# Reordering the per-unit work of a patch-attention tokenizer: value quarters before the score sums

## The reference, cut to what matters

```
reduce = mean over the 16 pixels of a patch               # 256 patches per image
q = layernorm(reduce) @ Wq.T                              # one query per patch
k, v = layernorm(pixels) @ Wkv.T                          # 16 keys and values per patch
attn = softmax(q * scale . k over the 16 pixels)          # 8 heads
token = reduce + (sum over pixels of attn * v) @ proj_w.T + proj_b
```

## Time and profile before

| what | value |
|---|---|
| median of 3 runs | 897.04 us (896.9 to 900.0) |
| the profiled execution's own time | 897.0 us |
| its span, first to last instruction | 895.2 us |
| granted TensorE clock, mean | 0.994 |
| PE busy | 844.0 us, 94% |
| DVE busy | 722.9 us, 81% |
| POOL busy | 523.4 us, 58% (work almost only in the tokenizer) |
| ACT busy | 494.1 us, 55% |
| tokenizer | to about 575 us of the span |

### The profile page before, as it was taken

The page is one execution under the profiler, slowest core; times in us unless marked ns, Lnnn a source line. Parts: engine busy times, 40 slices in busy tenths (PEclk is TensorE's granted clock), DMA queues, the critical chain, the costliest instruction groups (busy, mean ns, idle before and its releaser), DMA issues.

```text
span 895.2 us, 23485 instructions
## 1 busy us (share of the span) xinstructions
PE 844.0 (94%) x9144; PEld 354.2 (40%) x9144; DVE 722.9 (81%) x1189; ACT 494.1 (55%) x782; POOL 523.4 (58%) x387
## 2 busy tenths in 40 slices
PE   5799999999999999999999999798999999999996
PEld 1134434334334433433433434254344444444442
DVE  5688788788788788788788788895878878778775
ACT  3545555555545545545545546357766666666662
POOL 2789989989989989989989984200112111111110
PEclk9999999999999999999999999899999999999999
DMA  9588998998998998998998955200000000000000
GB/s 370 164 233 244 245 280 230 251 273 230 251 275 230 250 273 224 258 272 232 249 272 233 251 144 131 60 3 2 1 12 13 24 13 13 25 12 13 24 13 35
DMA packets 70560, 141.60 MB, mean 158 GB/s; under 512 B 5440, under 2 KB 5440, under 8 KB 69440
## 3 DMA queue, kind: packets, MB, share of 16 engines
q1 hardware_dynamic: 70464, 140.21, 54.9%
HBM read 68.88 MB, written 4.19 MB: 82 GB/s over the span
## 4 chain that ended last, share of the span: by engine, by line
PE 83%; DVE 7%; POOL 3%; DMA 3%; issue 2%; ACT 1%; SPq 1%; POOLq 0%; DVEq 0%
PE ring L956 24%; PE bank_ms L928 12%; PE bank_sq L928 6%; PE qp L995 6%; PE ring L1215 5%; DVE sb_prodk L1357 4%; PE ring L1185 4%; PE bank_ms L1227 3%; PE qp L916 2%; PE qp L1170 2%; DMA sb_arena<-x 2%; PE bank_sq L1215 2%; PE ring L1130 1%; PE bank_ms L1222 1%; PE bank_ms L1185 1%
## 5 line engine op out<-in xcount | busy, mean ns | idle before, releaser
L956 PE MATMUL ring<-sb_arena,sb_wqkv 64*64 64x512 f32 x2048 | 255.1, 601 | 5.2 <-DVE sb_prodv L1388 3.7
L1357 DVE TENSOR_TENSOR sb_prodk<-ring,sb_qbuf 128x1024 f32<-128x1024 f32 x128 | 153.3, 1220 | 18.5 <-PE ring L956 15.4
L653 POOL TENSOR_TENSOR sb_parts_q<-sb_arena,sb_const 128x512 fp32r<-128x512 f32 x15 | 15.6, 1039 | 244.8 <-DVE sb_arena L1593 194.4
L1388 DVE TENSOR_TENSOR sb_prodv<-ring,sb_wbc 128x1024 f32<-128x1024 f32 x128 | 151.0, 1202 | 1.9 <-issue 1.9
L497 POOL TENSOR_TENSOR sb_rows<-sb_arena 128x2048 f32<-128x2048 f32 x31 | 141.8, 4575 | 16.5 <-DMA sb_arena<-x 16.5
L697 ACT ACTIVATE sb_xsq<-sb_arena 128x2048 f32<-128x2048 f32 x64 | 118.4, 1896 | 3.4 <-DMA sb_arena<-x 3.4
L995 PEld LDWEIGHTS qp<-sb_prodv,sb_tok_w 64*64 64x64 f32 x3072 | 89.2, 133 | 59.9 <-issue 33.7
L956 PEld LDWEIGHTS ring<-sb_arena,sb_wqkv 64*64 64x64 f32 x2048 | 65.7, 132 | 119.0 <-issue 93.9
L995 PE MATMUL qp<-sb_prodv,sb_tok_w 64*64 64x128 f32 x3072 | 101.6, 271 | 3.1 <-POOL sb_prodv L604 1.8
L604 POOL TENSOR_TENSOR sb_prodv<-sb_prodv 128x256 f32<-128x256 f32 x128 | 93.2, 739 | 11.0 <-DVE sb_prodv L1388 11.0
L928 PE MATMUL bank_ms<-sb_prodk,sb_const 128*32 128x512 f32 x512 | 61.6, 598 | 14.9 <-DVE sb_prodk L1357 14.9
(11 more groups left out here) (248 smaller groups left out, 1467.1 us busy)
## 6 DMA issues: line engine op xcount, KB each, us to landing
sb_arena<-x SPq DMA_DIRECT2D x64, 1024.0 KB, 7.2
sb_wbc<-sb_wgt SPq DMA_DIRECT2D x256, 256.0 KB, 5.2
out<-sb_arena SPq DMA_DIRECT2D x16, 256.0 KB, 2.0
sb_rest_w<-rest_w SPq DMA_DIRECT2D x1, 950.5 KB, 22.1
sb_const<-const SPq DMA_DIRECT2D x1, 264.5 KB, 3.1
sb_tok_w<-tok_w SPq DMA_DIRECT2D x1, 260.5 KB, 2.9
sb_const<-const SPq DMA_DIRECT2D x1, 256.0 KB, 22.3
```

Source lines behind the costliest of these rows:

```text
L956: mm = pe.matmul(ring[slot][C * half:C * half + C, i, :], image_block(w, i), x[C * i:C * i + C, m, half, c], start=True, stop=True)
L1357: dve.tensor_tensor(by_pixel(prodk[:, c]), by_pixel(ring[c % 2][:, :, :]), q[:, :, None, :].to_broadcast([P, 2, N_PIX, G32]), ALU.mult).th ...
L1388: dve.tensor_tensor(prodv[:, :, :, G32 * c:G32 * (c + 1)], by_pixel(ring[k % 2][:, :, :]), by_pixel(wbc[:, c]), ALU.mult).then_inc(values_ ...
```

## The change

In each step of the tokenizer:

- PE: `values(n, 0)` and `values(n, 1)` stand ahead of `scores(n + 1)`; `pixel_squares(n + 2)` follows the scores directly; `values(n, 2)` and `(n, 3)` stand ahead of `query(n + 2)`; the 12 pixels of the projection are cut 6, 2 and 4 around the key quarters 2 and 3, not 4, 4 and 4.
- DVE: `pixel_var(n + 1)` is taken after the four key products (it stood at the end of the step before), the value products 0 and 1 come ahead of `score_scale` and `score_max`, `tokens` after them, and `query_scaled(n + 2)` is last.
- ACT: the squares of unit n+2 come ahead of `pixel_rstd(n + 1)`.
- POOL: `add_pixels(n, 2)` and `(n, 3)` end their own step; before, they stood in the next step, between the first and the second patch sum.

No instruction is added or taken away in a step. The diff, cut to its core:

```
 # POOL
                 if nxt2:
                     patch_sums_first(pool, n + 2, (m + 2) % NF)
-                if prev:
-                    add_pixels(n - 1, 2)
-                    add_pixels(n - 1, 3)
-                if nxt2:
                     patch_sums_rest(pool, n + 2)
...
                 if nxt:
                     norm_scores(n + 1)
+                add_pixels(n, 2)
+                add_pixels(n, 3)
 # ACT
+                if nxt2:
+                    squares(n + 2, (m + 2) % NF, 0)
+                    squares(n + 2, (m + 2) % NF, 1)
                 if nxt:
                     pixel_rstd(n + 1)
...
                 if nxt2:
-                    squares(n + 2, (m + 2) % NF, 0)
-                    squares(n + 2, (m + 2) % NF, 1)
                     take_means(n + 2, (m + 2) % NF)
 # PE
-                    project(n - 1, 0)
+                    project(n - 1, 0, 6)
                 if nxt:
                     keys(n + 1, m1, 2)
                 if prev:
-                    project(n - 1, 1)
+                    project(n - 1, 6, 8)
                 if nxt:
                     keys(n + 1, m1, 3)
                 if prev:
-                    project(n - 1, 2)
+                    project(n - 1, 8, N_SUM)
+                values(n, m, 0)
+                values(n, m, 1)
                 if nxt:
                     scores(n + 1)
-                values(n, m, 0)
-                values(n, m, 1)
                 if nxt2:
                     pixel_squares(n + 2, m2)
+                values(n, m, 2)
+                if nxt2:
+                    values(n, m, 3)
                     query(n + 2, m2)
+                    pixel_means(n + 2, m2)
...
 # DVE
             def step(n, m):
...
+                for c in range(NC):
+                    key_products(n + 1, m1, c)
+                pixel_var(n + 1)
                 value_products(n, m, 0)
                 value_products(n, m, 1)
...
+                score_scale(n + 1)
+                score_max(n + 1)
+                if prev:
+                    tokens(n - 1, mp)
+                value_products(n, m, 2)
+                score_sum(n + 1)
                 if nxt2:
                     query_var(n + 2)
...
+                score_inverse(n + 1)
+                value_products(n, m, 3)
                 if nxt2:
                     query_scaled(n + 2)
```

More of the change, by code:

```diff
@@ L988, in project @@
                     pe.wait_ge(weights_scaled, 4)
-                if part == N_SUM // N_PART - 1:
+                if hi == N_SUM:
                     pe.wait_ge(pixels_added, NC * u + NC)
-                for n in range(N_PART * part, N_PART * part + N_PART):
+                for n in range(lo, hi):
                     for i in range(2):
@@ L1063, in last_step @@
                 values(n, m, 0)
-                for part in range(N_SUM // N_PART):
-                    project(n - 1, part)
+                project(n - 1, 0, N_SUM)
                 values(n, m, 1)
@@ L1070, in last_step @@
                 drive(0, 3)
-                for part in range(N_SUM // N_PART):
-                    project(n, part)
+                project(n, 0, N_SUM)
             for n in range(UNITS - 1):
@@ L1499, in step @@
+                for c in range(NC):
+                    key_products(n + 1, m1, c)
+                pixel_var(n + 1)
                 value_products(n, m, 0)
                 value_products(n, m, 1)
-                if nxt:
-                    score_sum(n + 1)
+                score_scale(n + 1)
+                score_max(n + 1)
+                if prev:
+                    tokens(n - 1, mp)
+                value_products(n, m, 2)
+                score_sum(n + 1)
                 if nxt2:
@@ L1504, in step @@
                     query_var(n + 2)
-                if nxt:
-                    score_inverse(n + 1)
-                if not nxt:
-                    for level in range(3):
-                        far_steps(level)
-                value_products(n, m, 2)
+                score_inverse(n + 1)
+                value_products(n, m, 3)
                 if nxt2:
                     query_scaled(n + 2)
-                value_products(n, m, 3)
-                if nxt2:
-                    pixel_var(n + 2)
@@ L1516, in step, with last_step @@
-                if not nxt:
-                    for j in range(EARLY, BEFORE_TOKENS):
-                        scan_ahead(0, j)
-                        scan_on(0, j)
-            pipeline(dve, step, UNITS)
+            def last_step(n, m):
+                for j in range(1, EARLY):
+                    scan_ahead(0, j)
+                    scan_on(0, j)
+                tokens(n - 1, (m - 1) % NF)
+                value_products(n, m, 0)
+                value_products(n, m, 1)
+                for level in range(3):
+                    far_steps(level)
+                value_products(n, m, 2)
+                value_products(n, m, 3)
+                for j in range(EARLY, BEFORE_TOKENS):
+                    scan_ahead(0, j)
+                    scan_on(0, j)
@@ L1522, in _ @@
+            pipeline(dve, lambda n, m: last_step(n, m) if isinstance(n, int) and n == UNITS - 1 else step(n, m), UNITS)
             tokens(UNITS - 1, (UNITS - 1) % NF)
```

55 lines of the change are left out of this document (18 added, 37 removed).

## The result

The changed kernel takes 892.31 us (median of 5 runs, 891.54 to 893.5), the kernel before beside it 897.6 us (5 runs, 896.9 to 900.68). The ratio is 0.9928, with an interval of 0.9908 to 0.9948: faster by 0.7%, 5.3 us. The forecast was 883.0 us, a gain of 14 us. The range held the time, the size was wrong by more than half. That the range held is in part luck: the mixed case, by which the forecast was made, reached from 879 to 888 us, and only the always-late rival took the range as far as 892.

The account below looks back on a forecast made before the run. PE was taken to set the pace at 16.77 us per unit, POOL close behind. With early units at 16.1 and late ones at 16.65, taken as 16.3, 30 units save 14.1 us: 883 us, range 875 to 894.

Parts of the forecast that it names:

- the mixed case: Whole kernel: some units at the floor, others late through the loop; 883 us, reaching from 879 to 888; chance 0.62.
- the always-late rival: Steady units: the loop through the weight DMAs always binds, 16.65 us per unit, 893.4 us in all; chance 0.13.
- PE's wait and its shape changes: PE, each unit: 0.58 us wait before scores covered, four shape changes instead of six save 0.2 us; period 16.1 us.
- The floor of 16.1 us: Steady units: shortest period PE, POOL and DMA can keep; PE 16.1 us, POOL 16.05, DMA 15.1.
- The loop of 9.59 us plus the landing: DVE, POOL, SP, weight DMAs: 9.59 us plus norm-to-value-product time; 15.25 us in early units, 16.65 in late ones.
- The mixture: Steady units: 19 of 32 at 16.1 us, 13 at 16.65, giving 16.32, taken as 16.3 us per unit.
- The first unit and what follows the norm of unit 31 are taken as unchanged: Kernel's start and end: no gain or loss; all 14.1 us come from 30 units going from 16.77 to 16.3.
- the value products stand between it and its reader: DVE's moved pixel_var: rstd comes several us later but its reader is not held up; costed at nothing.
- ACT has squares ahead of it and is half idle: ACT, with rstd delayed by the moved pixel_var: room enough; costed at nothing, 0 to 0.1 us per unit.
- The cut 6, 2, 4 costs PE nothing: PE's projection around the key quarters: the new cut has the same 12 pixels, so no cost.
- Slower: Steady units: later weight landings, deciding from 7.2 us; at 7.6 us 17.25 us per unit, 911 us; chance 0.09.
- no late unit: Weight landings: if instruction fetch is mostly hidden, all are early, giving the first rival's sum, 877 us; chance 0.16.

Follow-up runs that it names:

- Experiments 4 and 9: Each against the changed kernel: 4, score_scale and score_max ahead of value product 1, 892.99 us; 9, add_pixels(n, 1) behind the norm, 889.58 us.
- experiment 1: Changed kernel with scale_out behind the first half's forcing in the last step, no longer ahead of expo(31): 890.32 us, ratio 0.9911 to the kernel before.
- experiment 3: Changed kernel with scale_out moved behind the forcing and the last step's projections cut at pixel 8: 886.99 us, ratio 0.9881 to the kernel before.
- experiment 8: Changed kernel with the projection cut into 4, 4 and 4 pixels as before: 895.41 us, ratio 0.9964 to the kernel before.
- experiment 7: Changed kernel with the loads of x of units 4 to 31 cut to 256 KB from 1 MB each: 894.34 us, ratio 0.9955 to the kernel before.

## Why the prediction was right in direction and wrong in size

- **PE's wait and its shape changes: right.** The wait before the scores is gone, the scores with the same shape behind them take 305.59 - 303.85 = 1.74 us, and no wait took its place at keys 2 or at value quarter 0.
- **The floor of 16.1 us: right, with its owner wrong.** Short units take 16.06 us. The forecast had PE at 16.1 and POOL at 16.05; it is POOL, whose two first patch sums are 16.06 us apart with no idle time but 0.16 and 0.28 us behind dependent results.
- **The loop of 9.59 us plus the landing: right.** 9.59 and 7.08 us were measured in the late unit shown, 16.67 for a forecast 16.65. Experiments 4 and 9 shorten it, and the long units vanish.
- **The mixture: right in kind, its share too low.** The two values that the forecast named are the ends of a spread: 9 of the 29 periods lie between 16.18 and 16.57 us, and the fourth landing makes some of the long ones. Of the 29 units from norm 1 to norm 30, 15 took more than 16.3 us (mean 16.70) and 14 less (mean 16.08), which gives 16.40. The forecast had 13 of 32 late and 16.3 us. That was rounded down from 16.32, and the share was counted in the kernel before, where the loop did not run. 29 x 0.1 = 3 us.
- **"The first unit and what follows the norm of unit 31 are taken as unchanged", and 30 equal units: wrong.** This is the step that failed: 2.5 + 2.1 = 4.6 of the 9.1 us come of edits in the last steps, 3.0 of the mis-sized mixture. Two edits reach into the last steps. The move of `pixel_var` was costed at nothing because "the value products stand between it and its reader". That holds for the reader, but not for `scale_out`, which stands behind `pixel_rstd` on ACT in step 30 and holds up `expo`: 3.2 us (experiment 1). "ACT has squares ahead of it and is half idle" is an average that says nothing of a step with 7.74 us more in it. And the projection in one block in `last_step`, whose rows were in the diff, got no term. The waits that came of both took the granted clock down, and the last `tokens` came 20.7 us after the norm in place of 18.5; with both edits repaired it is 17.5 (experiment 3). The 1.9 us behind that are not explained by the change.
- **"The cut 6, 2, 4 costs PE nothing": right, but it was worth 3 us** (experiment 8), as it lines keys 2 and 3 up with DVE's key products.
- **The rivals.** "Always late" gave 893.4 us, near the measured 892.3, but for a wrong reason: half of the units are short. "Slower" needed landings beyond 7.2 us; only one unit of the profile is well over it, with a fourth landing at 9.2 us and a period of 17.7 us. The slack that it leaned on, less idle time of the DMA engines, did not matter (experiment 7).

A rule of the Trainium skill was weighed in the forecast. By Runtime: NRT & Kernel Launch ("Instruction fetch mechanics") crossing a block is mostly hidden. The outcome that the forecast drew from it, no late unit, did not come: 15 of 29 are long. Whether the rule itself holds is open, since the packets as their cause are not shown.

## What to carry to other kernels

When an edit puts a DMA round trip between a unit and the next, add up the whole loop, from its landing through every engine back to its landing, and do it for each landing that something in the loop waits for; busy shares do not show it, and the timeline of before gives every term. Then read the first and the last steps apart from the steady ones: list what stands in them alone, and ask for each instruction that is moved what is queued behind it there. Orders of several engines that belong together are tried together, and what one engine's part of such an edit is worth is seen by undoing it in the finished kernel. A difference of some microseconds is placed by stretches before it is explained: here the part of the kernel that nobody had touched differed by up to 5.6 us between profiles.

## What the runs showed of the hardware that I had not expected

- A wait of some microseconds on PE can cost more than itself. After waits of 3.9 to 5.4 us the granted clock was between 0.50 and 0.70, and a projection of 96 matmuls took 5.40 us in place of 2.85. Over all fourteen profiles that last projection took 2.85 us where PE had waited up to 1.8 us for it (four profiles), and 4.2 to 5.4 us where it had waited 2.9 us or more (ten).
- The same instructions behind the same 2.2 us wait ran at a mean clock of 0.69 in one execution and 1.00 in another, a difference of 1.6 us.
- The landings of the eight spreading DMAs did not change with the loads beside them. With the loads of x at a quarter of their size and the data queue's share at 66.2% in place of 87.0%, the third of them still took 5.6 us from the norm in some units and 7.0 us in others.
- In the kernel before, the third landing comes 5.6 to 6.2 us or 6.9 to 7.6 us after the norm, with nothing between, and which of the eight DMAs is the first late one wanders from unit to unit. In the changed kernel 4 of 32 third landings lie between, at 6.4 to 6.8 us.
